# Linear attention on Trainium2: GpSimd's sum with beta waits for VectorE's clip of the group in front

## The reference

```
qh = split_heads(layernorm(q @ wq, gamma, beta))
kh = split_heads(layernorm(k @ wk, gamma, beta))      # k = v = context
vh = split_heads(layernorm(v @ wv, gamma, beta))
q_prime = relu(qh) + 1e-6
k_prime = (relu(kh) + 1e-6) * mask
kv  = einsum('bhnd,bhne->bhde', k_prime, vh * mask)
z   = 1 / (einsum('bhnd,bhd->bhn', q_prime, k_prime.sum(-2)) + 1e-6)
att = einsum('bhnd,bhde,bhn->bhne', q_prime, kv, z)
```

## Time and profile before

| | |
|---|---|
| median of 3 runs | 740.03 us (737.79 to 743.93) |
| profiled execution, its own time | 745.89 us |
| its span (first to last instruction) | 744.1 us |
| granted TensorE clock, mean | 0.970 |
| busy: PE, VectorE, ScalarE, GpSimd | 90%, 70%, 70%, 36% |
| instructions | 19421 |

### The profile page before, as it was taken

One profiled execution on the slowest core, in us unless ns is written; L12 is line 12 of the kernel. 1 busy time (PEld: TensorE's weight loads), 2 busy tenths in 40 slices (PEclk: granted clock), 3 DMA queues, 4 the chain that ended last, 5 costly groups with the idle time before them and its releaser, 6 DMA issues.

```text
span 744.1 us, 19421 instructions
## 1 busy us (share of the span) xinstructions
PE 666.2 (90%) x7317; PEld 467.4 (63%) x7317; DVE 522.7 (70%) x1228; ACT 519.2 (70%) x875; POOL 270.2 (36%) x324
## 2 busy tenths in 40 slices
PE   6888889885468999999999999999999987999997
PEld 5677778773225666666665566566666664577777
DVE  5898889978778779878878878878876751212112
ACT  6788889878326887887787787787888866634441
POOL 6788889882243214304322422432233100000000
PEclk9999999999589999999999999999999999799999
DMA  5122222525523476356547636645664480201110
GB/s 186 43 84 83 83 83 83 160 86 31 121 74 86 92 167 142 92 130 135 128 92 142 152 92 145 135 109 111 135 155 114 87 192 8 61 30 57 29 43 26
DMA packets 59523, 74.42 MB, mean 100 GB/s; under 512 B 35464, under 2 KB 40322, under 8 KB 59450
## 3 DMA queue, kind: packets, MB, share of 16 engines
q1 hardware_dynamic: 59450, 73.39, 41.8%
HBM read 32.35 MB, written 1.40 MB: 45 GB/s over the span
## 4 chain that ended last, share of the span: by engine, by line
PE 42%; issue 12%; DVE 10%; POOL 5%; ACT 2%; SPq 1%; DMA 1%; DVEq 0%; POOLq 0%; ACTq 0%
PE ps L832 7%; PE ps L844 7%; PE ps L771 7%; PE ps L683 6%; DVE mx L1694 6%; PE ps L758 5%; PE ps L669 3%; PE ps L675 3%; POOL Qb L1221 2%; POOL QD L1235 1%; ACT P L1096 1%; DVE kvall L1525 1%; POOL KP L1207 1%; PE ps L705 1%; SPq L450 1%
## 5 line engine op out<-in xcount | busy, mean ns | idle before, releaser
L1096 ACT ACTIVATE P<-ps,kbias,kscale 125x896 f32<-125x896 f32 x192 | 210.3, 1097 | 86.2 <-PE ps L758 83.4
L1694 DVE TENSOR_REDUCE mx<-ps 128x1 f32<-128x500 f32 x336 | 213.9, 671 | 46.4 <-PE ps L683 45.0
L683 PE MATMUL ps<-KP,Qb 128*128 128x500 bf16 x336 | 128.8, 385 | 15.1 <-DVE mx L1694 9.9
L1207 POOL TENSOR_TENSOR KP<-kvall,KP 128x1500 bf16<-128x1500 f32 x16 | 48.6, 3038 | 230.8 <-ACT KP L1039 230.8
L771 PE MATMUL ps<-P,Vp 125*32 125x112 f32 x3072 | 113.6, 265 | 2.7 <-ACT P L1096 1.4
L771 PEld LDWEIGHTS ps<-P,Vp 125*32 125x32 f32 x3072 | 67.4, 109 | 53.0 <-issue 37.8
L543 PE MATMUL ps<-wkv,cT 128*125 128x256 f32 x384 | 93.0, 386 | 4.9 <-ACT wkv L895 4.9
L543 PEld LDWEIGHTS ps<-wkv,cT 128*125 128x125 f32 x384 | 69.8, 191 | 13.7 <-ACT wkv L895 4.9
L1157 ACT ACTIVATE arena<-ps,b 128x448 f32<-128x448 f32 x64 | 40.4, 633 | 47.5 <-PE ps L832 41.6
L561 PE MATMUL ps<-arena 125*128 125x130 f32 x384 | 54.9, 285 | 17.5 <-DVE arena L1399 15.1
L758 PE MATMUL ps<-QS,KS 128*128 128x112 bf16 x768 | 68.7, 214 | 1.4 <-DVE QS L1700 1.4
(11 more groups left out here) (217 smaller groups left out, 1031.1 us busy)
## 6 DMA issues: line engine op xcount, KB each, us to landing
cT<-ctxT_dram SPq DMA_DIRECT2D x31, 750.0 KB, 4.1
KS<-KP SPq DMA_DIRECT2D x48, 375.0 KB, 7.3
arena<-KP SPq DMA_DIRECT2D x48, 375.0 KB, 7.2
QS<-QD SPq DMA_DIRECT2D x96, 28.0 KB, 5.5
wgu<-w_dram SPq DMA_DIRECT2D x8, 256.0 KB, 3.2
silu<-w_dram SPq DMA_DIRECT2D x8, 256.0 KB, 3.0
x<-xh_dram SPq DMA_DIRECT2D x1, 512.0 KB, 4.0
cT<-ctxT_dram SPq DMA_DIRECT2D x1, 500.0 KB, 5.3
```

The costliest lines, as they stand in the source:

```text
L683: ins = nc.tensor.matmul(ps[:, bank, 0:KCW], q[:, 128 * c:128 * c + 128], KP[par][0][:, KCW * k:KCW * k + KCW], start=True, stop=True)
L1096: nc.scalar.activation(P[t % 2][0:TK, :].rearrange("p (k n) -> p k n", k=2), src, ACT.Exp, scale=kscale[0:TK, bass.ds(n, 1)], bias=kbias[0 ...
L1207: nc.gpsimd.tensor_tensor(KP[par][2][:], krest, KP[par][1][:], ALU.subtract).then_inc(sem("kp3_ready"), 1)
L1694: ins = v.tensor_reduce(mx[:, c, k:k + 1], ps[:, bank, 0:KCW], AX.X, ALU.max)
```

## The change

GpSimd's sum with beta of group n gets one wait more: VectorE must have clipped the keys of group n-1 (`kp_ready` at n). Only the very first group has no such wait. Nothing else is changed.

```diff
@@ -1191,6 +1191,8 @@
                 nc.gpsimd.tensor_tensor(kn, kn, bc(row[0:TK, GAMMA, :], 1, [TK, GT, D]),
                                         ALU.mult).then_inc(sem("kg_ready"), 1)
                 pool.wait_ge(sem("kg_ready"), n + 1)
+                if not (first and k < 1):
+                    pool.wait_ge(sem("kp_ready"), n)
                 nc.gpsimd.tensor_tensor(kn, kn, bc(row[0:TK, BETA, :], 1, [TK, GT, D]),
                                         ALU.add).then_inc(sem("kb0_ready"), 1)
```

## The result

| | before | changed |
|---|---|---|
| median | 740.71 us (737.13 to 746.25, 10 runs) | 748.7 us (746.64 to 750.6, 10 runs) |
| profiled execution | 745.89 us, span 744.1 | 748.08 us, span 746.3 |
| granted TensorE clock, mean | 0.970 | 0.965 |
| last clip of the stage ends | 165.50 us | 166.77 us |

The ratio is 1.0102, interval 1.0076 to 1.0127: 8 us slower, where I had forecast 2.5 us faster (737.5 against the 740.03 us of the first three runs), and outside my range. The profiled executions differ by only 2.2 us. So there are two questions: why the changed kernel's profile is not at the 742.3 us of my sum, and why its medians are further apart than its profiles.

A forecast was written before the change was run, and what follows sets the result against it. GpSimd's own step and its stalls from clips meeting sums were taken to set the linear attention's pace. A 3.6 us gain from 745.9 gave 742.3 us profiled; less most of the 5.9 us offset, median 737.5 us, range 733 to 744.

The forecast's parts named there:

- the 742.3 us of my sum: Whole kernel, profiled execution: 745.9 us less the 3.6 us gained in the linear attention stage.
- the offset that I took off: Whole kernel: the profiled execution's 5.9 us above the 740.03 us median, carried over nearly whole to reach 737.5 us.
- the wait instruction itself I take at nothing: GpSimd ahead of the sum: the added wait costs nothing, being read while the clip is still 0.2 us from its end.
- My bound: The added wait on GpSimd: if not hidden, each 0.03 us of it would cost 41 x 0.03 = 1.2 us.
- my step of 3.03 us: GpSimd's time per group, gamma product to gamma product, after the change; 2.82 us before without a stall, 3.20 with them.
- The five lost pairs: Linear attention, 34 to 148 us: five of six pairs of batches where the sum held up the clip, 19.20 against 17.30 us.
- the 3.6 us that I wanted to win: Linear attention stage: 0.4 us before group 6 plus 4.1 over six pairs, less 0.9 in the last five groups.
- two or three stalled pairs less: Rival of nothing won: the usual run before has fewer stalled pairs than the profile, giving 740 to 743 us; chance 0.22.
- the 3.10 us case: GpSimd's step per group if a sum keeps the engine 1.30 us, judged by starts: gain only 0.7 us.
- ScalarE's loop: Sum to sum through ScalarE over two groups: 5.61 us, 6.05 once a pair, just fitting into 6.06 us.
- Clearly faster: Rival: the clip slips between the two GpSimd instructions at no cost, every pair 17.30 us, 730 us; chance 0.06.
- slower: Rival: the wait closes the ScalarE loop through GpSimd at the next group's small product, up to 747.3 us; chance 0.08.

The follow-up runs named there:

- before_a: The kernel before with no edit, profiled once more: 743.12 us in a single execution.
- before_b: The kernel before with no edit, profiled yet again: 742.4 us in a single execution.
- late_clip: The kernel before with a tiny memset on VectorE and a wait for it ahead of each clip: median 752.05 us, ratio 1.0115.
- swapped: The changed kernel with the sum's two waits in the other order, the clip's before the gamma product's: median 744.49 us, ratio 1.0025.
- clip_first: The kernel before, its sum of group n also waiting for VectorE's squares' sum of group n+1, in front of the clip: median 737.27 us, ratio 0.9983.
- after_b: The changed kernel with no further edit, measured again in a later comparison: median 748.41 us, ratio 1.0057.
- swapped_b: Repeat of swapped (the changed kernel with the clip's wait first) in a later comparison: median 745.48 us, ratio 1.0021.
- clip_first_b: Repeat of clip_first (wait for the squares' sum in front of the clip) in another comparison: median 737.15 us, ratio 0.9898.

## Why the prediction was wrong

From my 737.5 to the measured 748.7 us it is 11.2 us: 4.8 are the offset that I took off the profiled execution's 742.3 us, 5.8 are what the changed kernel's profiled execution took above those 742.3 us (2.5 of them the wait), and 0.6 lie between that execution and the median.

**The step that failed: "the wait instruction itself I take at nothing, since it can be read while the clip is still 0.2 us from its end".** It is not met ahead of the clip. It is the instruction that waits for the clip, and the sum comes behind it: 0.14 us from the clip's end instead of 0.08. My bound, 0.03 us for 1.2 us, had the right form, and 0.06 x 41 = 2.5 us would have been near the right size. Swapping the waits gave my step of 3.03 us to the hundredth, and took 2.9 us off the median. I had the cover wrong because I asked whether the wait could be *read* early, not which of the two waits stands alone.

**The second, larger in the median: "The profiled execution took 5.9 us more than the median", which I carried over nearly whole.** I had the mechanism in hand (an outcome within 0.04 us, 1.9 us a pair) and used it for one pair only. The offset was that mechanism: before_a and before_b lost three pairs and one, not five. The changed kernel, which always takes the same way, has an offset of -0.6 us (748.08 profiled, 748.7 median). With a fixed order an offset can still be larger, by the clock at least: late_clip's profiled execution, at 0.968, lies 2.6 us under its median. The five lost pairs of the profile were among the worst of the mixture, and the 3.6 us that I wanted to win from them were not there to win in the usual run. Had I carried no offset over, my own 742.3 us would have stood as the forecast of the median: 2.3 us slower than the 740.03 us I had, not 2.5 faster. I had "two or three stalled pairs less" as a rival at 0.22 but capped it at 743 us, as I let it act without the longer step.

**Smaller:** the start of the stage (0.5 of its 1.6 us; the other 1.1 is the landing of the input, which varied from 9.67 to 11.01 us over all executions here), 0.22 to 0.24 us instead of 0.14 once a pair, 0.24 us in the first pair, and 0.9 us behind the stage, where 577.9 us (at a mean clock of 0.968) to 581.2 us (at 0.959) were seen in all kernels. In a stage where GpSimd's step sets the pace the late start is not made up: with it left out, changed kernel and swapped repeat to 0.1 us (155.90 to 155.97, 152.43 and 152.44).

**What held:** that the change does what it says; that the clip ends 0.29 us behind gamma; the 1.27 us of the sum, in its duration and its starts, against the 3.10 us case, whose number came true while its reason did not; that ScalarE's loop fits in (swapped has the same loop and ran at 3.03); pairs all alike. "Clearly faster", at 730 us, had the right picture of a clip ahead of the sum, and clip_first is that version. Its gain of 9.9 us over the profiled execution was nearly right as well (the last clip ends at 155.96 instead of 165.50 us, the profiled execution is 737.54 us instead of 745.89); only taken from the median of 740 us it gave 730 instead of 737, by the same offset. For "slower" I had the wrong mechanism, and one wrong number: I wrote that nothing is gained from a loop of 6.40 us on, but that is the lost pair's 3.20 us a group, while the 41 groups took 127.6 us, 3.11 us each; the bound was 6.2 us.

**The size of the loss in the end:** the 8 us of the result became 5.3 us in the second comparison, because the kernel before had a median of 743.06 us there and not 740.71; the changed kernel's hardly moved (748.7 and 748.41). In that comparison the changed kernel lies 11.3 us above clip_first, and 10 us of it are in the stage by the traces (166.91 against 156.72 us for the last clip). The kernel before lies in between, 5.9 us above clip_first and 5.3 below the changed one. Waiting for a clip's *end* each time puts 0.36 to 0.43 us of idle time into each group, and removes a stall that only part of the pairs had.

**Open:** after_b lies 11.3 us and swapped_b 8.3 us above clip_first_b by the medians, where I had expected 8.5 and 5.5 from the six pairs alone. For swapped_b it is 6.6 us by the end of the last clip in the traces (5.55 from the six pairs, 0.95 behind group 42, 0.07 before group 6); the profiled executions lie 6.4 us apart. The rest is where each stands to its own median: swapped_b was profiled at a clock of 0.965, 1.2 us under its median, clip_first_b at 0.960, 0.7 us above.

clip_first_b reaches gamma of group 6 25.8 us behind ScalarE's first squares, clip_first 24.2 us, and before_b 26.6 us where before_a took 24.9. The traces show a lower granted clock there: PE's query projection (L518) and the table from 14 to 18 us (columns as in the earlier trace rows, the clock is the third figure from the end), first in clip_first_b, then in clip_first:

```profile
15.05 2.04 PE L518 MATMUL ps<-wq_sb,xT 128*128 128x128 f32 x8 [2.04 <-ACT xT L904]
14.00:18.00 4.00, 2.94 (x11) 2.79 (x12) 2.99 (x5) 3.82 (x11) 3.80 (x5) 0.63 0.46 174
```

```profile
15.92 1.13 PE L518 MATMUL ps<-wq_sb,xT 128*128 128x128 f32 x8 [2.14 <-ACT xT L904]
14.00:18.00 4.00, 2.08 (x14) 1.97 (x15) 3.28 (x5) 3.72 (x12) 3.69 (x4) 1.00 0.59 192
```

The same eight matmuls take 2.04 us where the clock is at its lower level (1.2 GHz) for a part of the stretch, and 1.13 us at the full one (2.4 GHz), and ScalarE's squares of the third group then wait for PE's projection. In before_b it is 0.76 and 1.87 us; in the eleven other traces the clock is 1.00 there. What lowers it in these two is open.

Why the pair without stalls is 17.3 us was not tried: clip_first gives its sum a later start in nearly every group (0.16 us behind gamma's end, not 0.08) and still takes 17.3 us, so GpSimd's step does not set it, and PE, at 17.0 us busy, is the nearest candidate by its row alone.

## What to carry to other kernels

Where two engines meet at a shared resource within hundredths of a us, one profile shows one outcome of many: look at the spread of the runs first, and compare runs of equal granted clock; take a repeated profile if there is one, and do not subtract a single profile's offset from a kernel whose order will be fixed. To fix an order, wait for the instruction *in front of* the competitor's, not for the competitor's end: the first cost nothing here, the second 0.36 to 0.43 us of idle time in each group. Where an instruction has several waits, look in the trace which of them becomes an instruction of its own, and let that be the one that is met first.

## What the hardware showed that I had not expected

- Of two waits on one GpSimd instruction the last written stood as an instruction of its own, and a wake-up through it took 0.14 us, against 0.08 us through the sum's own wait: 0.06 us a group, 2.9 us in the kernel.
- A wait already met left the gap in front of the sum at 0.08 us, but where a register instruction stood on its line the sum came 0.07 us later, enough to turn the outcome of every pair.
- An instruction can start up to 0.02 us behind another in the trace and still go first: the clip won 0.01 us behind the sum at 61.96 and 0.02 behind at 121.33, and lost 0.02 behind it at 64.13. By 0.03 us behind it lost each time.
- The clip with an accumulator took 0.68 to 0.69 us in all 48 groups, beside GpSimd or not.
- In one kernel, runs at a mean granted clock of 0.970 and 0.958 lay 4 us apart.
